# A new planned order, two short scans, shorter gate arithmetic and dummy products on TensorE in a twelve-sublayer decoder

## What is computed

```python
x = _layernorm(x + _L0_attn_ref(x, ...))                 # state space ("mamba")
x = _layernorm(x + _L0_xattn_ref(x, ctx, ctx, ...))      # attention 0
x = _layernorm(x + _L0_ffn_ref(x, ...))                  # attention 1, then experts 0
x = _layernorm(x + _L1_attn_ref(x, ...))                 # attention 2 (wide values)
x = _layernorm(x + _L1_xattn_ref(x, ctx, ...))           # attention 3
x = _layernorm(x + _L1_ffn_ref(x, ...))                  # experts 1
x = _layernorm(x + _L2_attn_ref(x, ...))                 # attention 4, causal
x = _layernorm(x + _L2_xattn_ref(x, ctx, ctx, adj, mask, ...))  # attention 5, masked
x = _layernorm(x + _L2_ffn_ref(x, ...))                  # experts 2, hidden width 512
x = _layernorm(x + _L3_attn_ref(x, ...))                 # linear attention
x = _layernorm(x + _L3_xattn_ref(x, ctx, ...))           # attention 6, gathered rows
x = _layernorm(x + _L3_ffn_ref(x, ...))                  # experts 3
```

```python
def step(h, inputs):
    u_t, dt_t, B_t, C_t = inputs
    A_bar = jnp.exp(dt_t[:, :, None] * A[None, :, :])
    h = A_bar * h + (dt_t[:, :, None] * B_t[:, None, :]) * u_t[:, :, None]
    return (h, jnp.sum(h * C_t[:, None, :], axis=-1) + D * u_t)
```

## Time and profile before

| | |
|---|---|
| median of 3 runs | 1449.04 us (1448.42 to 1449.28) |
| the profiled execution's own time | 1452.28 us |
| its span, first to last instruction | 1450.6 us |
| PE, DVE, ACT, POOL busy | 1195.1, 987.1, 703.2, 282.0 us |
| mean granted TensorE clock | 0.891 of full speed |

### The profile page before, as it was taken

The page is one execution under the profiler, slowest core; times in us unless marked ns, Lnnn a source line. Parts: engine busy times, 40 slices in busy tenths (PEclk is TensorE's granted clock), DMA queues, the critical chain, the costliest instruction groups (busy, mean ns, idle before and its releaser), DMA issues. The chain is left out here.

```text
span 1450.6 us, 24473 instructions
## 1 busy us (share of the span) xinstructions
PE 1195.1 (82%) x8092; PEld 798.2 (55%) x8092; DVE 987.1 (68%) x2547; ACT 703.2 (48%) x1507; POOL 282.0 (19%) x395
## 2 busy tenths in 40 slices
PE   6766777789888988997586669999958999888898
PEld 4222343457575745684243346788835767664566
DVE  3997775666787776547268887533368999845555
ACT  4443566555434456653255435422235556545553
POOL 3455122001111010012021100000015445311000
PEclk7886798799999988998699678999988999999899
DMA  6004222013312130134422100210000001032111
GB/s 202 29 0 130 76 81 78 20 60 91 115 56 78 45 122 12 60 93 161 155 68 78 63 31 24 77 30 23 1 16 1 2 1 31 19 106 64 59 64 40
DMA packets 69066, 89.23 MB, mean 62 GB/s; under 512 B 5960, under 2 KB 52048, under 8 KB 67152
## 3 DMA queue, kind: packets, MB, share of 16 engines
q1 hardware_dynamic: 68944, 87.67, 18.8%
HBM read 63.46 MB, written 23.72 MB: 60 GB/s over the span
## 5 line engine op out<-in xcount | busy, mean ns | idle before, releaser
L1297 ACT ACTIVATE P<-bank 128x512 f32<-128x512 f32 (+1 forms) x448 | 229.5, 596 | 112.4 <-PE bank L1022 95.8
L1646 DVE TENSOR_REDUCE mx<-bank 128x2 f32<-128x512 f32 x320 | 195.0, 684 | 63.1 <-PE bank L998 63.1
L1097 PE MATMUL bank<-xT,room 128*128 128x256 f32 x640 | 167.6, 396 | 0.4
L1457 POOL TENSOR_SCALAR rstd<-mv 128x2 f32<-128x2 f32 x56 | 13.9, 248 | 766.3 <-DVE mv L1508 662.8
L1106 PE MATMUL bank<-room 128*128 128x256 f32 x640 | 162.5, 392 | 0.0
L1097 PEld LDWEIGHTS bank<-xT,room 128*128 128x128 f32 x640 | 122.5, 197 | 23.5 <-issue 4.7
L1035 PE MATMUL bank<-P,V 128*32 128x256 f32 (+1 forms) x1536 | 123.2, 450 | 12.6 <-ACT P L1297 11.1
L1106 PEld LDWEIGHTS bank<-room 128*128 128x128 f32 x640 | 121.8, 196 | 20.9 <-issue 3.6
L1022 PE MATMUL bank<-QKR 50*128 50x256 bf16 (+1 forms) x896 | 85.5, 288 | 44.1 <-DVE mx L1646 14.7
L998 PE MATMUL bank<-QKR 48*128 48x256 bf16 (+1 forms) x896 | 83.5, 299 | 36.2 <-ACT P L1297 8.5
L1785 DVE TENSOR_TENSOR room<-bank,room 128x512 f32<-128x512 f32 x64 | 44.2, 691 | 93.9 <-PE bank L1097 93.8
(11 more groups left out here) (231 smaller groups left out, 2307.0 us busy)
## 6 DMA issues: line engine op xcount, KB each, us to landing
QKR<-split_rows SPq DMA_DIRECT2D x112, 192.0 KB
room<-gate_rows SPq DMA_DIRECT2D x64, 256.0 KB, 3.8
split_rows<-parts SPq DMA_DIRECT2D x56, 192.0 KB, 2.3
split_rows<-parts SPq DMA_DIRECT2D x56, 128.0 KB, 1.9
room<-in_w SPq DMA_DIRECT2D x6, 1024.0 KB, 7.3
room<-in_w SPq DMA_DIRECT2D x3, 2048.0 KB, 14.4
split_rows<-parts SPq DMA_DIRECT2D x56, 64.0 KB, 1.7
room<-in_mask SPq DMA_DIRECT2D x4, 512.0 KB, 4.4
```

Source lines behind the costliest of these rows:

```text
L1097: last = nc.tensor.matmul(bk[:, j * S:(j + 1) * S], w[:, e, (2 * f + j) * 128:(2 * f + j + 1) * 128], x, start=True, stop=True)
L1297: nc.scalar.activation(P[:, (e - 1) % NBUF_P, 0:width], psum(st, p)[:, 0:width], ACT.Exp, scale=SCALE).then_inc(read[k], 1)
L1646: V_.reduce_max(to, sc[:, :].rearrange("p (t s) -> p t s", t=TPB), AX.X).then_inc(read[k], 1)
```

## The change

Four things are changed together.

1. Two short scans: `abar` is written in full (512 columns, no zero column), and DVE scans each batch entry of 256 columns by itself. The exponential becomes a step of its own, `MX`; `MX`, `MB` and `MC` are separate chains.
2. The gate arithmetic on DVE handles both tiles of a batch entry and both picks at once through a tensor `picks` of 128 x 32, in place of a loop.
3. A new order: new entries in `COST`, `LANDING` and `FAVOUR`, and `PIPE`, which the planner adds after each PE part.
4. Dummy products: where the planner's clock has PE idle for more than `FILL_OVER` = 1.5 us before the next PE step, a step `FILL` stands ahead of it, with as many products as fit in 0.7 of that gap at 0.22 each. Each is the bf16 identity (128 x 128) times the identity repeated to 512 columns, written to a bank that the planner holds free; nobody reads it.

```diff
-    "MB": ((PE, 0.22), (ACT, 0.72), (DVE, 2.2)), "MC": ((PE, 0.22), (ACT, 0.66)), ...
+    "MX": ((ACT, 0.72),), "MB": ((PE, 0.25), (DVE, 2.1)), "MC": ((PE, 0.25), (ACT, 0.62)), ...
-LANDING = {"RL": 2.2, "ROWS": 2.3, "SHIFT": 2.2, "GB": 2.2, "GL": 2.5, "LD": 14.0, "LW": 4.0}
+LANDING = {"RL": 2.1, "ROWS": 4.2, "SHIFT": 3.2, "GB": 2.2, "GL": 2.5, "LD": 14.0, "LW": 4.0}
+PIPE = 0.2
+FILL, FILL_OVER, FILL_ONE = 0.7, 1.5, 0.22
...
-FAVOUR = {"P2": 0.4, ... "MG": 0.9, ... "DT": 2.7, ... "GL": -0.6, ... "GBb": 1.5}
+FAVOUR = {"P2": 0.4, ... "MG": 0.8, ... "DT": 0.9, ... "GL": 3.0, ... "GBb": 1.5, "XB": -1.3, ... "GLc": 3.9}
...
         _, t, j, st = best
         heads[j] += 1
+        if cost(st)[0][0] == PE and t - free[PE] > FILL_OVER:
+            fills = int(FILL * (t - free[PE]) / FILL_ONE)
+            at = min(range(8), key=lambda i: until[i])
+            if fills and until[at] <= free[PE]:
+                filler = ("FILL", len(listed), fills)
+                place[filler, 0] = at
+                free[PE] += FILL_ONE * fills
+                listed.append(filler)
...
-            t = max(t, free[eng]) if i == 0 else max(t + HOP, free[eng])
+            t = max(t, free[eng]) if i == 0 else max(t + HOP + PIPE * (cost(st)[i - 1][0] == PE), free[eng])
...
                 if k in PSUM_STEPS:
                     for j in range(banks_of(st)):
-                        if held[st, j]:
+                        if held[st, j] and held[st, j][0][0] != "FILL":
...
+                if k == "FILL":
+                    for _ in range(st[2]):
+                        nc.tensor.matmul(bk[:, :], identb[:, :], identb[:, :].unsqueeze(1).to_broadcast([128, 4, 128]), start=True, stop=True, skip_group_check=True)
...
-                    later, steps_in = (x.rearrange("p (b s) -> p b s", s=S)[:, :, 1:S] for x in (abar[:, i % 2, :], dt[:, 512 * c:512 * (c + 1)]))
-                    nc.scalar.activation(later, steps_in, ACT.Exp, scale=negA[:, n:n + 1]).then_inc(abar_done, 1)
+                    nc.scalar.activation(abar[:, i % 2, :], dt[:, 512 * c:512 * (c + 1)], ACT.Exp, scale=negA[:, n:n + 1]).then_inc(abar_done, 1)
...
-                    V_.tensor_tensor_scan(hs[:, (i - 1) % 2, :], abar[:, (i - 1) % 2, :], bu[:, (i - 1) % 2, :], 0.0, ALU.mult, ALU.add).then_inc(scan_done, 1)
+                    for b in range(2):
+                        part = slice(b * S, (b + 1) * S)
+                        last = V_.tensor_tensor_scan(hs[:, (i - 1) % 2, part], abar[:, (i - 1) % 2, part], bu[:, (i - 1) % 2, part], 0.0, ALU.mult, ALU.add)
+                    last.then_inc(scan_done, 1)
...
+                    every = iota[:, 0:NE].unsqueeze(1).unsqueeze(1).to_broadcast([128, TPB, 2, NE])
+                    link(V_.tensor_tensor(picks[:, :, :, :], every, top_atf[:, :, 0:2].unsqueeze(3).to_broadcast([128, TPB, 2, NE]), ALU.is_equal))
+                    if m == 0:
+                        link(V_.tensor_tensor(chosen[:, TPB * b:TPB * (b + 1), :], picks[:, :, 0, :], picks[:, :, 1, :], ALU.add))
...
-                    for t in range(TPB):
-                        g = gates[:, TPB * b + t, :]
-                        link(V_.tensor_scalar(g, iota[:, 0:NE], top_atf[:, t, 0:1], gs[:, t, 0:1], ALU.is_equal, ALU.mult))
-                        link(V_.tensor_scalar(gtmp[:, :], iota[:, 0:NE], top_atf[:, t, 1:2], gs[:, t, 1:2], ALU.is_equal, ALU.mult))
-                        link(V_.tensor_tensor(g, g, gtmp[:, :], ALU.add))
...
-                    V_.tensor_copy(gtmp[:, :], gtmp[:, :]).then_inc(gates_done, 1)
+                    link(V_.tensor_tensor(picks[:, :, :, :], picks[:, :, :, :], gs[:, :, 0:2].unsqueeze(3).to_broadcast([128, TPB, 2, NE]), ALU.mult))
+                    V_.tensor_tensor(gates[:, TPB * b:TPB * (b + 1), :], picks[:, :, 0, :], picks[:, :, 1, :], ALU.add).then_inc(gates_done, 1)
```

More of the change, by code:

```diff
@@ L60 @@
[L60 to L64, removed]
@@ L65 @@
[L65 to L67 removed]
+    "BIAS": ((DVE, 1.15),), "SM": ((PE, 0.24), (DVE, 1.25)), "MS": ((DVE, 0.36),), "MT": ((PE, 0.15), (ACT, 0.3)), "SHIFT": ((SP, 1.3),),
@@ L80, in cost @@
     if st[0] == "SM" and st[1] == MASKED:
-        return ((PE, 0.24), (DVE, 1.85))
+        return ((PE, 0.24), (DVE, 1.9))
     if st[0] == "P2" and st[1] == CAUSAL:
@@ L117, in lanes @@
 def lanes():
-    layers = range(7)
-    units = [(a, b) for a in layers for b in range(B)]
+    units = UNITS
     mamba = [("DT", 0), ("DT", 1), ("BC", 0), ("DZ", 0), ("DZ", 1), ("DL", 0), ("DL", 1), ("BC", 1)]
@@ L186, in at @@
     def at(n):
-        return n // B, n % B
+        return UNITS[n]
     def narrow_before(n):
@@ L212, in needs @@
         back = [(i % NSTATE, i // NSTATE)] if i >= 0 else []
-        if k in ("MB", "MC"):
+        if k == "MX":
+            return [("DL", c)] + [("MB", *x) for x in back]
+        if k == "MB":
+            return [("MX", n, c), ("BC", c)] + [("ME", *x) for x in back]
+        if k == "MC":
             return [("DL", 1 if k == "MC" else c), ("BC", c)] + [("ME", *x) for x in back]
@@ L275, in needs @@
         if k == "V":
-            return ([("GM", b)] if a == GATHERED else x_of(SUB_OF[("attn", a)], b)) + ([("PV", *back, 3)] if back and back[0] != SELF_WIDE else [])
+            return ([("GM", b)] if a == GATHERED else x_of(SUB_OF[("attn", a)], b)) + [("PV", *at(j), 3) for j in range(n - 2, -1, -2) if at(j)[0] != SELF_WIDE][:1]
         if k == "SM":
@@ L335, in needs @@
         i = B * m + b - 2
-        return [("MO", m, b, *expert_units(m)[-1])] + ([("YT", *at(i))] if i >= 0 else [])
+        return [("MO", m, b, *expert_units(m)[-1])] + ([("YT", i // B, i % B)] if i >= 0 else [])
     if k == "YT":
@@ L496, in plan @@
             free[eng] = t
+        t += PIPE * (cost(st)[-1][0] == PE)
         if takes_bank(st):
@@ L1615, in _ @@
                     full(dve, st)
-                    if n >= 2 and units[n - 2][1] != SELF_WIDE:
-                        full(dve, ("PV", units[n - 2][1], units[n - 2][2], 3))
+                    for j in [j for j in range(n - 2, -1, -2) if units[j][1] != SELF_WIDE][:1]:
+                        full(dve, ("PV", units[j][1], units[j][2], 3))
                     for t in range(TPB):
```

67 lines of the change are left out of this document (37 added, 30 removed), and 3 rows, old and new, of the table UNITS.

## The result

The changed kernel takes 1409.39 us (median of 4 runs, 1406.66 to 1414.16), the kernel before 1448.73 (median of 4, 1447.68 to 1449.28): a ratio of 0.9733, 95% interval 0.9705 to 0.9761. One ratio is known to some 3 to 6 us, so a difference of two of them under about 5 us is not told from none. DVE's lines for scores and gates are 29 higher in the changed kernel (L1646 is L1675).

The account below looks back on a forecast made before the run. No engine was full (PE 82%, DVE 68%); PE bound some stretches, DVE others. Terms 3 - 6 - 7 + 3 = -7 took 1452.3 to 1445.3, by the median 1442 us (chance 0.43); range 1420 to 1474.

Parts of the forecast that it names:

- short scans: Scan loop on DVE, 32 rounds: two scans of 256 cost 0.1 us more each, +3 us, bounds 0 and 5.5.
- the load's stall: PE's 17.35 us stall at the load of experts 2's weights: some 7 us of work moves into it, -7.
- the rest of the order: All other order changes, with cover changing by a few steps at a time: 0 us, with 10 either way.
- gates: Sixteen expert gates on DVE: DVE loses about 16 us, of which 6 shows at the end, -6 us.
- dummies: 559 dummy products on PE: +14 in PE stretches, +9 elsewhere, -20 by the clock, together +3 us.
- The bound of 12: Gates: the upper limit of their gain, which was put between 0 and 12 us.
- half of the low time: Clock's return: half of PE's time at 1.2 GHz goes, 61 us of PE's time, a third waited for, -20 us.
- PE's own stretches: Stretches where PE is nearly always busy: 129 dummies, 28 us, half of it charged, +14 us.
- The other signs: What would show the forecast: mean clock 0.93 or more, dummies busy about 125 us, PE idle some 180.
- the dummies delay PE: Rival: dummies push real work back more than the clock returns, slower, 1470 us; chance 0.30.
- the clock pays in full: Rival: all the low clock time goes, -40 beside +23 for the dummies and -10, 1422 us; chance 0.14.
- it cancels: Rival: the stall at the load stays its full length, leaving -6, +3 and +3, 1449 us; chance 0.13.

Follow-up runs that it names:

- e13: Changed kernel without dummy products, with the gates and the one long scan of before, so the new order alone: 1439.18 us, ratio 0.9946.
- e18: Changed kernel without dummy products and with the old gates; new order and short scans stay: 1440.76 us, ratio 0.9952.
- e1: Changed kernel without its 559 dummy products; new order, short scans and new gates stay: 1419.55 us, ratio 0.9807.
- e5: Changed kernel with the gate arithmetic of before, nothing else: 1427.87 us, ratio 0.9853.
- e4: Kernel before with the new gate arithmetic, nothing else: 1436.07 us, ratio 0.993.
- e8: Changed kernel with 820 dummy products instead of 559, at the same 80 places: 1431.54 us, ratio 0.9892.
- e7: Changed kernel with 259 dummy products instead of 559, at the same 80 places: 1413.36 us, ratio 0.977.
- e10: Changed kernel with only the 392 dummies at 59 places where PE waited under 0.5 us in the kernel without dummies: 1415.12 us, ratio 0.9769.
- e17: Changed kernel with 430 dummies, leaving out the 129 in stretches where PE of the kernel before was nearly always busy: 1409.99 us, ratio 0.9742.
- e11: Changed kernel with only 167 dummies where PE waited 0.5 us or more without dummies, and the 32 at the start: 1416.84 us, ratio 0.9787.
- e9: Changed kernel with 475 dummies at 92 places, set by PE's waits over 0.8 us in the trace without dummies: 1406.0 us, ratio 0.9703.
- e2: Kernel before, in its own order, with 465 dummy products by the same rule, nothing else: 1443.04 us, ratio 0.9978.
- e16: Kernel before with the load of the weights of experts 2 in six parts of 1 MB behind later rows and shifts: 1432.3 us, ratio 0.9891.

## Why the prediction was wrong

By its own terms, each beside what the runs gave:

| term | predicted | measured |
|---|---|---|
| short scans | +3 | +1 (e13 to e18), +2.5 by DVE's time in the scans |
| the load's stall and the rest of the order | -7 and 0 | -8 together (e13) |
| gates | -6 | -21 (e18 to e1), -17 with dummies (e5), -10 on the old order (e4) |
| dummies | +3 | -10 (e1) |
| sum | -7 | -39 |

**The gates are the step that failed most.** The prediction put "DVE loses about 16 us, 1 us a gate", and then took 6 of it since "it shows only where the gate is waited for or DVE is the bound". Both halves were off. DVE lost 22 us of busy time and the pauses between some 75 operations, not 16: the sixteen gates are 29 us shorter, on the old order too (78.2 and 49.4 us in e4). And the gate is waited for: the first product that needs it stands in PE's queue with nothing to overtake it, and the row maxima stand behind it in DVE's. The program had the hint: the old gates of experts 0 carry two more operations per tile than the three lines that were priced. The bound of 12 was itself too narrow. On the old order 10 counted, on the new one 17 to 21. Why the new order gets more out of the same saving was not tried; that it was planned with a cost of 3.5 instead of 4.5 for a gate would fit, and is only argued.

**The dummies are the second.** The prediction had +3 and the runs have -10. The clock came back further than "half of the low time": 115 us of the changed span are at 1.2 GHz (2 x 0.041 x 1406.8) against 316, and PE's real work fell by 68 to 82 us, not 61. Two sizes then stood against each other: a third of the returned time was to be waited for, and the products cost 23. Two runs fix two unknowns, if both prices are straight lines. From e1 to the changed kernel, 80.4 us of PE's work returned (1193.0 to 1112.6), 136.1 of dummies, -10. From e1 to e8, 89.1 returned, 193.4 of dummies, +12. These give 1.07 us gained per us returned and 0.55 lost per us of dummies. By these, e7 (43.6 and 76.0 on its page) makes -5 as measured, e10 (55.4 and 101.4) -3 against -5 measured, e17 (61.0 and 107.3) -6 against -9, e11 (31.7 and 53.9) -4 against -3. But e9 (71.5 and 125.2) would make -8 and has -15, e2 on the old order (56.2 and 120.2) +6 and has -3, and a returned microsecond can't well gain more than itself. The rows of e1 and e8 behind this:

```profile
PE 1193.0 (84%) x8092; PEld 794.0 (56%) x8092; DVE 971.5 (68%) x2502; ACT 708.0 (50%) x1509; POOL 284.5 (20%) x395
```

```profile
PE 1297.3 (91%) x8912; PEld 836.5 (59%) x8912; DVE 975.2 (68%) x2502; ACT 708.8 (50%) x1509; POOL 284.1 (20%) x395
```

So the straight lines are not the truth. With them both sides were too small by far, some -86 for -20 and some +75 for +23. A price that rises as the gaps fill up would leave both nearer to what was predicted, and no run tells the two apart: how large the gain and the cost are each stays open. What is shown is the net (e1), that more dummies turn it round (e8), and that the 129 in PE's own stretches cost nothing on balance (e17).

**The load's stall** was read rightly in its mechanism: one wait instead of two, 7.56 us where about 10 were expected. "About 7 us, which moves into the hole" fits the -8 of the order alone, though the wait fell by 10 to 11 us, so the match is in part luck. e16 adds that the whole stall was worth 16, so a longer step was there to take.

**The rest of the order** at 0, with 10 either way, is not contradicted. **The scans** held: starts 2.53 us apart, 2.6 expected. The Trainium skill (VectorE: DVE Perf Modes, "The TRN2 errata") speaks against the short scans; the estimate from it was 5.0 us. The traces have 2.5 us more of scans in all, so the measurement decides for the smaller number.

The other signs: clock 0.959 (0.93 or more), dummies busy 136 us (125), PE idle 158 (180). The up steps around seven dummies at the third entry of experts 1 are 1.5 us longer, as expected: 8.6 us in the changed kernel from the first to the eighth, 7.07 in e1.

```profile
614.27 1.03 PE L1125 MATMUL bank<-xT,room 128*128 128x256 f32 x4
615.13 1.67 PE L940 MATMUL bank<-identb 128*128 128x512 bf16 x7
616.64 6.21 PE L1125 MATMUL bank<-xT,room 128*128 128x256 f32 x28
```

```profile
621.09 7.07 PE L1125 MATMUL bank<-xT,room 128*128 128x256 f32 x32
```

So the delay that was charged is real at such a place, and the net of all places is what the charge missed. Waits of DVE for scores did not take the place of PE's: 41.3 us against 63.1 before and 44.3 without dummies. They begin to at 820 dummies.

Of the rivals, that the dummies delay PE (1470, 0.30) is what e8 shows, but on a kernel with 261 more. That the clock pays in full (1422) had most of the clock right; but its gain was the smaller part of the result. That it cancels (1449) fell with its premise: the stall did not stay at 17.35 us. The range of the prediction ends at 1474 where its slowest rival is worked out to 1470; nothing hangs on that. The advice of the Trainium skill (TensorE: Matmul & The Clock Gate, "Why this matters for your kernels") to leave TensorE no long idle between bursts agrees with the clocks measured here; what filling the idle costs can take all of the gain or more, by e2 and e8.

## What to carry to other kernels

A chain of small operations that a product at the head of TensorE's queue waits for is priced from its whole length, pauses included, also in a stretch where TensorE looks full: here 29 us of it were worth 10, 17 and 21 us. Count its operations from the program, not from three lines of a list. Dummy products can pay or cost: beside none, 559 brought 10 us and 820 cost 12. Measure both sides, and ask of each stretch not how far its clock is down but how much sooner its last product is done: the stretch with the largest rise of the clock became 0 to 4 us shorter. A large load is cut up and spread over the queue's pauses, so that small transfers with somebody waiting need not stand behind it.

## What the runs showed of the hardware

- The mean clock is not free to buy: 0, 199, 259, 392, 559 and 820 dummies gave 0.891, 0.915, 0.924, 0.929, 0.959 and 0.964 in the profiled executions (others of one kernel differ by up to 0.011). The time of the last is worse by 22 us than that of the one before it.
- A DVE operation on 128x8 with two operands per partition takes 0.29 us, one on 128x32 with broadcast operands 0.19. Four times the elements, and shorter. In the changed kernel, by time order:

```profile
269.59 0.19 DVE L1773 TENSOR_TENSOR picks<-picks,gs 128x32 f32<-128x32 f32 x1
```

- A small transfer behind the load waits for it. The stores of parts in the changed kernel between 640 and 705 us (192 KB and less) took 12.4 us from issue to landing at the most, with the 6 MB ahead of them, and 1.6 at the least; one issue alone held SyncE 8.2 us where the median is 0.49. The Trainium skill (DMA: Bandwidth & Descriptors, "Two DMAs through the same engine are not ordered") says that descriptors within one queue of a DMA engine start in order; the trace agrees: the last of the load landed at 680 us (20.7 after its issue), the first stores behind it, issued at 666, at 679.

```profile
L805 SPq DMA_DIRECT2D split_rows<-parts x24: 360/486/8166, 649.5 to 699.9; - x24
...
DMA to landing us min/median/max: 1.6/3.1/12.4
```
